# Phase-memory attention stage: mean taken off the first FFN weights, cross products on VectorE, phases behind the retrieval

## What is computed

```python
magnitude = sigmoid(x @ W_mag.T + b_mag) * 5.0
phi = random_phases * position * 0.01
cos_phi, sin_phi = cos(phi), sin(phi)
weighted = magnitude * x
mem_r, mem_i = cumsum(weighted * cos_phi), cumsum(weighted * sin_phi)
inv_sqrt = 1.0 / sqrt(cumsum(magnitude) + 1e-08)
mr, mi = mem_r * inv_sqrt, mem_i * inv_sqrt
phi_q = phi + x @ W_q.T + b_q
cq, sq = cos(phi_q), sin(phi_q)
context = concatenate([x * cos_phi, x * sin_phi, mr * cq + mi * sq, mi * cq - mr * sq])
h = (context - mean(context)) / sqrt(var(context) + 1e-05) * ln_g + ln_b      # over 512 features
out = gelu(h @ W1.T + b1) @ W2.T + b2
x_stream = x_stream + (x + out)
```

## Time and profile before

| what | value |
|---|---|
| median of three runs | 1878.57 us (1877.64 to 1880.87) |
| the profiled execution, its own time | 1873.64 us |
| its span, first to last instruction | 1871.9 us |
| the stage `L2Attend`, from its first instruction on VectorE to its last add | 1096.95 to 1216.89 us |
| PE, DVE, ACT, POOL busy over the span | 87%, 68%, 62%, 32% |
| mean granted TensorE clock over the span | 0.956 |

### The profile page before, as it was taken

How to read it: one execution, slowest core, us unless ns; L and a number is a source line. 1 busy time by engine, 2 the same in 40 slices (tenths; PEclk the granted TensorE clock), 3 DMA queues, 4 the chain that set the end, 5 groups by cost and what they waited for, 6 DMA issues and landing times.

```text
span 1871.9 us, 40552 instructions
## 1 busy us (share of the span) xinstructions
PE 1628.6 (87%) x15460; PEld 865.6 (46%) x15460; DVE 1278.7 (68%) x2625; ACT 1163.1 (62%) x2729; POOL 590.2 (32%) x739
## 2 busy tenths in 40 slices
PE   6999989898898989889588965869899997799998
PEld 2556355633456345633244322324455462355546
DVE  5875687546786488647475668547788764788876
ACT  4666466643666566646266664464788766388875
POOL 3651265202653065300474004223233101332310
PEclk9999999999999999999689988996999999699999
DMA  5000000000000000000541000015653100554410
GB/s 199 19 19 7 6 19 19 7 0 1 19 19 13 0 19 19 14 1 0 102 89 28 1 1 0 1 35 102 133 99 94 19 1 6 115 94 101 90 30 23
DMA packets 53870, 73.31 MB, mean 39 GB/s; under 512 B 5616, under 2 KB 38608, under 8 KB 53168
## 3 DMA queue, kind: packets, MB, share of 16 engines
q1 hardware_dynamic: 53680, 70.73, 17.2%
HBM read 44.46 MB, written 16.88 MB: 33 GB/s over the span
## 4 chain that ended last, share of the span: by engine, by line
PE 56%; ACT 14%; DVE 12%; issue 8%; POOL 6%; DMA 2%; DVEq 0%; SPq 0%; POOLq 0%; ACTq 0%
PE ps L197 52%; ACT arena L709 6%; DVE arena L801 2%; DVE arena L845 2%; ACT arena L1614 2%; PE ps L588 1%; ACT arena L270 1%; ACT arena L272 1%; POOL arena L945 1%; PE ps L1508 1%; DMA arena<-arena 1%; DVE arena L933 1%; POOL arena L944 1%; ACT arena L265 1%; DVE arena L1654 1%
## 5 line engine op out<-in xcount | busy, mean ns | idle before, releaser
L197 PE MATMUL ps<-arena 32*64 32x128 f32 (+7 forms) x10984 | 650.9, 302 | 57.8 <-ACT arena L1614 18.8
L197 PEld LDWEIGHTS ps<-arena 32*64 32x64 f32 (+4 forms) x10984 | 364.6, 118 | 340.7 <-issue 118.1
L197 PE MATMUL ps<-arena,w_L0f 128*128 128x512 f32 (+3 forms) x992 | 369.0, 507 | 31.1 <-DVEq L2835 9.3
L1614 ACT ACTIVATE arena<-ps 128x512 f32<-128x512 f32 (+1 forms) x640 | 333.3, 576 | 84.6 <-PE ps L197 76.1
L1654 DVE TENSOR_REDUCE arena<-ps 128x2 f32<-128x512 f32 x512 | 322.9, 684 | 87.4 <-PE ps L197 85.4
L709 ACT ACTIVATE arena<-ps,arena 128x128 f32<-128x128 f32 x512 | 226.7, 461 | 68.3 <-DVE arena L847 66.7
L197 PEld LDWEIGHTS ps<-arena,w_L0f 128*128 128x128 f32 (+2 forms) x992 | 174.6, 188 | 158.4 <-issue 98.9
L197 PE MATMUL ps<-arena,const 128*128 128x512 f32 (+2 forms) x532 | 171.8, 608 | 62.2 <-DVE arena L2136 22.1
L952 POOL TENSOR_TENSOR arena<-arena 128x512 f32<-128x512 f32 x128 | 132.5, 1042 | 154.8 <-DVE arena L831 154.5
L801 DVE TENSOR_TENSOR arena<-ps,arena 128x1024 f32<-128x1024 f32 x128 | 151.8, 1205 | 14.8 <-ACT arena L723 9.2
L723 ACT ACTIVATE arena<-ps 128x512 f32<-128x512 f32 x128 | 76.8, 600 | 100.4 <-DVE arena L801 77.7
(11 more groups left out here) (252 smaller groups left out, 2114.8 us busy)
## 6 DMA issues: line engine op xcount, KB each, us to landing
scratch<-arena SPq DMA_DIRECT2D x40, 384.0 KB, 2.8
arena<-scratch SPq DMA_DIRECT2D x80, 192.0 KB
arena<-scratch SPq DMA_DIRECT2D x80, 128.0 KB
arena<-arena SPq DMA_DIRECT2D x64, 128.0 KB, 2.4
arena<-scratch SPq DMA_DIRECT2D x80, 88.0 KB
w_L0f<-in_L0f SPq DMA_DIRECT2D x2, 1557.0 KB, 12.8
arena<-in_experts SPq DMA_DIRECT2D x8, 256.0 KB, 8.4
arena<-arena SPq DMA_DIRECT2D x80, 12.0 KB
```

The costliest lines, as they stand in the source:

```text
L197: return self.nc.tensor.matmul(o, lhsT, rhs, start=start, stop=stop, skip_group_check=True)
L1614: S.activation(self.pt[g % 4][:, e, 0:both], ps[:, self.shifted_bank(2 * g + e), 0:both], ACT.Exp, scale=self.scale).then_inc(self.exped.s ...
```

## The change

- **Mean off the weights.** The four column sums of the gained weights `w1` are taken on PE once (four products of 256 columns with the constant mean matrix), and VectorE subtracts the mean from `w1` in `center_weights` (four instructions of 256 columns, PSUM and SBUF in, beside the two small bias additions). `hidden` is then the product of these centred weights with the uncentred context. The centred context is still written, into `sqb`, for the squares alone; the squares are taken in place there.
- **Cross products.** mi\*sq and mr\*sq move from GpSimd to VectorE, inside the retrieval. GpSimd keeps four products per chunk.
- **VectorE's order.** Round n is now retrieval of n, weights of n+1, steady of n-1, add of n-2, phases of n+1, centring of n. Ahead of the loop weights of 0 come before phases of 0, phases of 0 no longer wait for ScalarE's first sines, and phases of 1 no longer stand ahead of retrieval 0.
- **PE's order.** The four magnitude projections come before the four query projections. Round n is the mean of n, the first half of hidden of n, the contraction of n-1, the second half of hidden of n, the variance sum of n; in the last round the variance sum comes before the second half. The contraction waits for each gelu apart.
- **ScalarE.** The magnitude's inverse root of chunk 0 comes before the sines of chunk 0; in round n magnitude of n+1 and the sines of n+1 come first, then squares, deviation and gelu of n, with table sets loaded ahead of their use.

The diff, cut to its core:

```diff
     def tensor(self, eng, ch):
...
         for c in range(NCHUNK):
             self.norm.wait_done(eng, c)
-            mm(ps[:, 2 * c, :], k.wp("L2", "magT"), self.h[:, chunk(c)])
+            mm(ps[:, 2 * c, :], k.wp("L2", "magT"), self.h[:, chunk(c)]).then_inc(self.measured.sem, 1)
+        for c in range(NCHUNK):
             mm(ps[:, 2 * c + 1, :], k.wp("L2", "qT"), self.h[:, chunk(c)]).then_inc(self.projected.sem, 1)
...
+        for i in range(4):
+            m = mm(ps[:, 6, FF:2 * FF], k.K("mean"), self.w1[:, i, :], start=i == 0, stop=i == 3)
+        m.then_inc(self.weights_summed.sem, 1)
+        for n in range(NCHUNK):
+            self.wait_ge(eng, self.carried, n + 1)
+            self.wait_ge(eng, self.retrieved, n + 1)
+            self.wait_ge(eng, self.centred, 4 * n)
+            for i in range(4):
+                m = mm(ps[:, 0, :], k.K("mean"), self.ctxb[n % 2][:, i, :], start=i == 0, stop=i == 3)
+            m.then_inc(self.averaged.sem, 1)
+            self.expand(eng, n, 0)
+            if n:
+                self.contract(eng, n - 1)
+            if n == last:
+                self.sum_squares(eng, n)
+            self.expand(eng, n, 1)
+            if n < last:
+                self.sum_squares(eng, n)
+        self.contract(eng, last)
...
     def phases(self, eng, ch, n):
...
-        self.wait_ge(eng, self.sined, n + 1)
+        if n:
+            self.wait_ge(eng, self.sined, n + 1)
...
+    def center_weights(self, eng):
+        k, V = self.k, self.k.nc.vector
+        self.wait_ge(eng, self.weights_summed, 1)
+        for o in range(2):
+            m = V.tensor_tensor(self.bias1[:, o:o + 1], k.ps[:, 6, o:o + 1], k.C(f"L2_b1_{o}"), ALU.add)
+        m.then_inc(self.bias_ready.sem, 1)
+        for i in range(4):
+            m = V.scalar_tensor_tensor(self.w1[:, i, :], k.ps[:, 6, FF:2 * FF], -0.25, self.w1[:, i, :], ALU.mult, ALU.add)
+        m.then_inc(self.w1_ready.sem, 1)
...
+    def retrieve(self, eng, ch, n):
...
+        ch.did(TT(ctx[:, 2, :], self.mr, cq, ALU.mult))
+        TT(self.cross[1], self.mr, sq, ALU.mult)
+        self.wait_ge(eng, self.scaled, n + 1)
+        TT(self.cross[0], self.mi, sq, ALU.mult).then_inc(self.crossed.sem, 1)
+        ch.wait_ge()
+        ch.did(TT(ctx[:, 3, :], self.mi, cq, ALU.mult))
+        self.wait_ge(eng, self.crossed, n + 1)
+        TT(ctx[:, 2, :], ctx[:, 2, :], self.cross[0], ALU.add)
+        ch.wait_ge()
+        TT(ctx[:, 3, :], ctx[:, 3, :], self.cross[1], ALU.subtract).then_inc(self.retrieved.sem, 1)
+
+    def centre(self, eng, n):
+        ctx, V = self.ctxb[n % 2], self.k.nc.vector
+        self.wait_ge(eng, self.averaged, n + 1)
+        self.wait_ge(eng, self.summed, n)
+        for i in range(4):
+            V.scalar_tensor_tensor(self.sqb[:, i, :], self.k.ps[:, 0, :], 0.25, ctx[:, i, :], ALU.mult, ALU.subtract).then_inc(self.centred.sem, 1)
...
     def vector(self, eng, ch):
...
+        self.weights(eng, 0)
         self.phases(eng, ch, 0)
-        self.weights(eng, 0)
...
+        self.center_weights(eng)
+        self.wait_ge(eng, self.sined, 1)
+        for n in range(NCHUNK):
+            self.retrieve(eng, ch, n)
+            if n + 1 < NCHUNK:
+                self.weights(eng, n + 1)
+            if n:
+                self.steady(eng, n - 1)
+            if n > 1:
+                self.add(eng, n - 2)
             if n + 1 < NCHUNK:
                 self.phases(eng, ch, n + 1)
...
+            self.centre(eng, n)
+        self.add(eng, NCHUNK - 2)
+        self.steady(eng, NCHUNK - 1)
         self.add(eng, NCHUNK - 1)
 
     def gpsimd(self, eng, ch):
...
             self.wait_ge(eng, self.hidden, 2 * (n - 1))
+            self.wait_ge(eng, self.centred, 4 * (n - 1))
             G.tensor_tensor(seqs(ctx[:, 0, :]), seqs(hc), table(self.cphi), ALU.mult)
             G.tensor_tensor(seqs(ctx[:, 1, :]), seqs(hc), table(self.sphi), ALU.mult).then_inc(self.carried.sem, 1)
-            self.wait_ge(eng, self.scaled, n + 1)
-            self.wait_ge(eng, self.sined, n + 2)
-            self.wait_ge(eng, self.retrieved, n)
-            G.tensor_tensor(self.cross[0], self.mi, self.sq[n % 2], ALU.mult)
-            G.tensor_tensor(self.cross[1], self.mr, self.sq[n % 2], ALU.mult).then_inc(self.crossed.sem, 1)
```

More of the change, by code:

```diff
@@ L2004, in sines, with magnitude, square, deviation @@
         S.activation(cos_out, cos_out, ACT.Sin, bias=self.quarter, scale=-1.0).then_inc(self.sined.sem, 1)
+    def magnitude(self, eng, n):
+        k, S = self.k, self.k.nc.scalar
+        self.wait_ge(eng, self.accumulated, n + 1)
+        S.activation(self.am, self.am, ACT.Ln, bias=k.C("eps8"), scale=5.0).then_inc(self.am_logged.sem, 1)
+        self.wait_ge(eng, self.am_logged, n + 1)
+        S.activation(self.am, self.am, ACT.Exp, scale=-0.5).then_inc(self.am_ready.sem, 1)
+    def square(self, eng, n):
+        for i in range(4):
+            self.wait_ge(eng, self.centred, 4 * n + i + 1)
+            self.k.nc.scalar.activation(self.sqb[:, i, :], self.sqb[:, i, :], ACT.Square).then_inc(self.squared.sem, 1)
+    def deviation(self, eng, n):
+        k, S = self.k, self.k.nc.scalar
+        self.wait_ge(eng, self.summed, n + 1)
+        self.wait_ge(eng, self.steadied, 2 * n)
+        S.activation(self.dev, k.ps[:, 1, :], ACT.Ln, bias=k.C("eps5"), scale=0.25).then_inc(self.dev_logged.sem, 1)
+        self.wait_ge(eng, self.dev_logged, n + 1)
+        S.activation(self.dev, self.dev, ACT.Exp, scale=-0.5).then_inc(self.dev_ready.sem, 1)
+    def gelu(self, eng, n):
+        self.wait_ge(eng, self.bias_ready, 1)
+        for o in range(2):
+            self.wait_ge(eng, self.steadied, 2 * n + o + 1)
+            self.k.nc.scalar.activation(self.hb[:, o, :], self.hb[:, o, :], ACT.Gelu, bias=self.bias1[:, o:o + 1]).then_inc(self.gelued.sem, 1)
     def scalar(self, eng, ch):
@@ L2041, in scalar @@
-            if n < NCHUNK:
+            self.square(eng, n)
+            S.preload_act_table_set("natural_log_exp_and_others")
+            self.deviation(eng, n)
+            S.preload_act_table_set("gelu_and_others")
+            self.gelu(eng, n)
+            if n + 1 < NCHUNK:
                 S.preload_act_table_set("natural_log_exp_and_others")
@@ L2137, in vector @@
-            if c >= 0:
-                self.wait_ge(eng, self.dev_ready, c + 1)
-                self.wait_ge(eng, self.down, c)
-                for o in range(2):
-                    self.wait_ge(eng, self.hidden, 2 * c + o + 1)
-                    V.scalar_tensor_tensor(self.hb[:, o, :], ps[:, 2 + o, :], -1.0, self.dev, ALU.mult, ALU.mult).then_inc(self.steadied.sem, 1)
-            if n + 1 < NCHUNK:
-                self.weights(eng, n + 1)
-            if c >= 1:
-                self.add(eng, c - 1)
+            self.centre(eng, n)
```

162 lines of the change are left out of this document (63 added, 99 removed).

## The result

The changed kernel took 1860.43 us (median of four runs, 1858.15 to 1861.85) against 1878.11 of the kernel before in the same comparison (1874.14 to 1880.87): ratio 0.9905, 95% interval 0.9885 to 0.9925, 17.7 us less. The profiled execution took 1859.11 us, its span 1857.4 against 1871.9.

The account below looks back on a forecast made before the run. The stage was taken as a VectorE chain up to retrieval 3, then a chain mostly through PE. Head 10.4 less 3.0 in the rounds plus 5.3 at the end gives 12.7 us: 1865.9 us, range 1859 to 1872 (forecast's own 1862 to 1870).

Parts of the forecast that it names:

- rival with less meeting: GpSimd's products fall beside VectorE instructions that read PSUM, so fewer are stretched; 1859.6 us, chance 0.10.
- part 3: Rounds, retrieval to retrieval: 19.3 us each with GpSimd's stretch, 57.9 against 54.9 for three, so 3.0 us given back.
- part 1: Head, up to the first scan: earlier weights and phases of chunk 0, weights' centring done at 1118.1, scan held 0.7.
- part 4: End, from retrieval 3 to the last add: PE runs 16.8 us without a stop; 20.4 instead of 25.7, 5.3 us saved.
- reading as turns: VectorE instructions fed from SBUF and GpSimd products exclude each other, holding 1.09 or 1.26 us per product; PSUM readers pass freely.
- sign that L2080 and L2082 would both pass 1.3 us: Two phases instructions on VectorE, in the rounds, would each be stretched by GpSimd's products to over 1.3 us.
- Part 2: A retrieval, with cross products on VectorE: 7.1 us instead of 8.3; retrieval 0 ends 10.4 us earlier.
- In the rounds that is worth nothing, since PE has slack: Weights' centring frees hidden from waiting for centring and squares; worth nothing in rounds, PE's 16.8 us being under VectorE's 19.3.
- Meeting: GpSimd products stretching VectorE instructions; rival with more: four full turns per round or moved products worthless, 1869.9 to 1871.6, chance 0.14.
- The clock: Rival: PE's clock stays at half speed through rounds after its idle stretch, 14.2 us lost per chunk; slower, chance 0.04.

Follow-up runs that it names:

- product_more: Changed kernel plus a fifth GpSimd product per chunk whose result nobody reads; stage 107.43 us against 103.55, ratio to before 0.9942.
- centre_first: Changed kernel with centring ahead of the phases on VectorE and squares ahead of the sines on ScalarE from round 1 on; stage 101.53 us, ratio 0.9875.
- cross_back: Changed kernel with the two cross products returned from VectorE to GpSimd; stage 109.45 us against 103.55, ratio to before 0.9925.
- warm: Changed kernel plus ten unread PE products of 128x512 in the idle stretch ahead of retrieval 0; stage 103.56 us, ratio to before 0.9887.
- warm_centre_first: Changed kernel plus ten unread PE products ahead of retrieval 0 and centring ahead of the phases in all rounds; stage 103.79 us, ratio 0.9909.
- mean_contexts_centre_first: Changed kernel with the mean taken off the contexts again, and centring and squares first from round 1 on; stage 111.61 us, ratio 0.9957.

## Why the prediction was right, and where it was off

- **Sum.** Forecast 12.7 us and 1865.9; measured 16.4 in the stage and 17.7 between the medians. The median, 1860.43, lies in the range of 1859 to 1872 but near its lower edge, below the forecast's own 1862 to 1870, and close to the 1859.6 of the rival with less meeting. The 1.3 us beyond the stage's gain can't be told from the movement of what surrounds it, so that much of the median's gain may be chance. The direction and the signs of the three parts (head, rounds, end) held; the size was too small by 3.7 in the stage: 2.6 in part 3, 0.8 in part 1, 0.3 in part 4.
- **Part 3, the mis-sized term.** "Turn by turn the phases end 9.8 us after the retrieval": the centring behind them began 8.6, 9.0 and 9.2 us after it. The stretch is 2.7, 1.9 and 1.4 us, 6.0 in all, where the text had 8.4. I let each turn cost a whole product, 1.09 or 1.26; a full one costs 0.95 in the rows, and product_more measures the same 0.95 per product by itself. The earlier trace rows had it already: L2051 at 1.63 against 0.69 for its like is 0.94. Why it is less than the product's own length no run shows. The reading as turns stands: centre_first, which puts readers of PSUM beside the products, took the stretch away. The sign that L2080 and L2082 would both pass 1.3 us held in round 1 alone.
- **Part 1.** 11.2 instead of 10.4: stretches of 1.6 and 0.8 instead of 2.1 and 0.7, centrings of the weights at 0.33 instead of 0.4. The wait for the sines was real: putting it back costs 2.9. The order of the projections on PE and that of the inverse root and the sines on ScalarE were not undone alone, so what they give of the head stays open.
- **Part 2.** A retrieval takes 7.1, as worked out; cross_back gives the 1.1 per chunk (1.0 forecast).
- **Part 4.** 20.1 instead of 20.4. Without the order of the last round it is 3.7 longer.
- **"In the rounds that is worth nothing, since PE has slack" was wrong.** The slack of 16.8 against 19.3 is there for hidden only because it needn't wait for centring, which the same change put last on VectorE. With hidden behind centring, rounds 1 and 2 grew by 8.3 us and the end by 8.6, in part through the slow variance sums. In this order of VectorE the two belong together: with the mean on the contexts it gives nothing (0.9995). With centring ahead of the phases from round 1 on, the mean on the contexts keeps 8.3 us of the gain (111.61 against 119.94). The mean off the weights alone, in the old order, was not run.
- **The rivals.** Meeting was less than forecast, but not absent. The clock didn't cost the changed kernel anything that shows: its first mean took 6.53 us, with the granted clock at 0.50 until 1129, but warm shows that it is off the path, and in rounds 1 and 2, with gaps of 1.2 to 1.9 us, the clock stayed at 1.00. As a mechanism it shaped seven of the experiments.
- The parts don't add: undoing five of them one at a time costs 5.9, 8.1, 16.8, 3.7 and 2.9, 37 us against a gain of 16.4, because an undoing opens gaps on PE that the others close, as the rows of the first four show.

## What to carry to other kernels

Count VectorE's instructions between two points of the chain, then ask which of them read PSUM: here those ran bare beside GpSimd's work, and putting them there was worth 2.0 us. When work is moved later on one engine, look for who reads its result: algebra that removes that reader's wait can pay although it adds instructions, as the mean taken off the weights once does here. And where PE is nearly the bound, a schedule that shortens another engine's round may open an idle gap on PE whose half clock costs more than was saved, as in warm_centre_first; read the granted clock behind every gap.

## What the hardware showed that was not expected

PE's granted clock behind idle gaps was not expected. Behind gaps of 1.0 to 1.9 us in the rounds the means took 3.7 us, full speed. Behind 2.97, 3.24, 3.53, 3.59 and 4.00 us in five kernels the next four products took 5.12, 6.76, 6.39, 6.66 and 6.25 us. The gap's length doesn't decide alone: four products took 3.70 us behind 3.24 in the kernel before and behind 2.91 in mean_contexts_centre_first, and 5.40 behind only 1.90 in warm. What decides no run here shows. The Trainium skill, TensorE: Matmul & The Clock Gate, section Loop structure matters more than you think, warns that a long wait between matmuls makes PE run cold. The five kernels agree, with 1.4 to 3.1 us lost on four products.

That the stage repeats within 0.02 us while the execution around it moves by over 10 us was not expected either: an edit worth 2 us can be read from the stage where the whole run's interval, 0.2 to 0.3% to each side, can't show it.
